# Attribute sums of a graph layer in groups of 32 nodes: two edges a product, destinations gathered and transposed

## The reference, cut to what matters

```python
h = jnp.maximum(_layernorm(x, axis=-1), 0.0)
x = x + _L0_gnn_ref(h, edge_index, W1, b1, W2, b2)     # two convolutions with D^-1/2 A D^-1/2
h = jnp.maximum(_layernorm(x, axis=-1), 0.0)
agg = jax.ops.segment_sum(edge_attr, col, num_segments=x.shape[0])   # (206250, 64) -> (6250, 64)
h = jnp.concatenate([h, agg, u[batch]], axis=1)        # then w1, w2, w3 with leaky relu
```

## Time and profile before

| | us |
|---|---|
| median of 3 runs | 1436.68 (1434.59 to 1437.53) |
| the profiled execution | 1436.67 |
| its span | 1435.0 |
| first stage | 0 to 148 |
| attribute stage | 148 to 415 |
| later stages | 415 to 1435 |

### The profile page before, as it was taken

One profiled execution on the slowest core, in us unless ns is written; L12 is line 12 of the kernel. 1 busy time (PEld: TensorE's weight loads), 2 busy tenths in 40 slices (PEclk: granted clock), 3 DMA queues, 4 the chain that ended last, 5 costly groups with the idle time before them and its releaser, 6 DMA issues. The chain is left out here.

```text
span 1435.0 us, 31864 instructions
## 1 busy us (share of the span) xinstructions
PE 1133.5 (79%) x10325; PEld 749.0 (52%) x10325; DVE 886.2 (62%) x1543; ACT 484.0 (34%) x1067; POOL 203.8 (14%) x170
## 2 busy tenths in 40 slices
PE   0012089999925889999999998549999999999974
PEld 0001089999924566666666664224444444444443
DVE  7575698888828979999999991621222222222221
ACT  0024100000006778888888882410111111111111
POOL 5710610000013922111111000300000000000000
PEclk9999999999966989999999999759999999999975
DMA  8423379999820545665446665959477777777400
GB/s 192 149 68 98 94 232 288 286 285 283 262 58 14 187 142 197 219 218 181 163 167 219 211 200 185 318 180 345 140 227 232 231 229 228 234 224 228 112 14 11
DMA packets 231891, 270.89 MB, mean 189 GB/s; under 512 B 31003, under 2 KB 202565, under 8 KB 231662
## 3 DMA queue, kind: packets, MB, share of 16 engines
q1 hardware_dynamic: 137258, 173.78, 39.5%
q10 hardware_dynamic: 89904, 81.89, 17.2%
q0 software_dynamic: 4688, 14.70, 3.3%
HBM read 178.73 MB, written 91.61 MB: 188 GB/s over the span
## 5 line engine op out<-in xcount | busy, mean ns | idle before, releaser
L779 ACT CAST adj_all<-win_p 128x392 f32 x784 | 346.9, 497 | 44.7 <-PE win_p L829 22.9
L829 PEld LDWEIGHTS win_p<-mv,st 128*128 128x128 f16 x3136 | 213.4, 100 | 141.8 <-ACT adj_all L779 21.7
L829 PE MATMUL win_p<-mv,st 128*128 128x98 f16 x3136 | 256.2, 211 | 17.9 <-ACT adj_all L779 10.7
L727 DVE TENSOR_TENSOR st<-iota_lo,code 128x2048 f16 x196 | 241.2, 1230 | 32.8 <-ACT code L768 13.2
L1369 PE MATMUL dense_p_b<-adj_all,g_hi 128*128 128x512 f16 (+1 forms) x637 | 232.2, 372 | 18.7 <-SPq L1127 16.6
L543 PE MATMUL agg_p<-ahot,arows 128*64 128x64 f32 x3724 | 218.8, 223 | 34.5 <-DVE ahot L584 34.5
L844 PE MATMUL dense_p<-adj_all,g_hi 128*128 128x448 f16 x686 | 241.5, 352 | 1.2 <-DVE total L738 0.8
L844 PE MATMUL dense_p<-adj_all,g_lo 128*128 128x448 f16 x686 | 242.1, 353 | 0.0
L543 PEld LDWEIGHTS agg_p<-ahot,arows 128*64 128x64 f32 x3724 | 218.7, 139 | 34.6 <-DVE ahot L584 34.6
L1369 PE MATMUL dense_p_b<-adj_all,g_lo 128*128 128x512 f16 (+1 forms) x637 | 232.1, 371 | 0.0
L727 DVE TENSOR_TENSOR mv<-iota_mv,code 128x1568 f16 x196 | 190.8, 973 | 0.0
(11 more groups left out here) (162 smaller groups left out, 1017.6 us busy)
## 6 DMA issues: line engine op xcount, KB each, us to landing
adj_d<-adj_all ACTq DMA_DIRECT2D x14, 5488.0 KB, 19.4
adj_all<-adj_d SPq DMA_DIRECT2D x11, 6272.0 KB, 23.5
arows<-in_edge_attr_dram SPq DMA_DIRECT2D x98, 608.0 KB, 3.6
adj_all<-adj_d SPq DMA_DIRECT2D x7, 896.0 KB, 9.9
disb<-dis_d SPq DMA_DIRECT2D x24, 256.0 KB, 4.9
hT_d<-hT ACTq DMA_DIRECT2D x12, 256.0 KB, 2.8
cur<-hT_d SPq DMA_DIRECT2D x12, 256.0 KB, 7.5
h1T_d<-total SPq DMA_DIRECT2D x12, 256.0 KB, 6.5
```

The costliest lines, as they stand in the source:

```text
L727: ins = nc.vector.tensor_tensor(hot[:, bass.ds((b * BG + j) % 2, 1), u, :, :] .rearrange("p a w (n t) -> p (a w) n t", t=2), iota[:, :].re ...
L779: nc.scalar.copy(adj[:, bass.ds(b % 2, 1), :, bass.ds(j * GN + k * WN, WN)] .rearrange("p b h d -> p (b h) d"), win_p[:, k % 4, 0:WP * MV] ...
L829: ins = nc.tensor.matmul(win_p[:, k % 4, 0:WP * MV] .rearrange("p (h c t) -> p h c t", c=WP, t=PN)[:, :, c, :], st[:, odd, k // UW, pair, ...
```

## The change

Groups have 32 nodes (196 of them, GA) and AC = 9 x 128 = 1152 edges, with a tenth column of zeros. A product takes two of a partition's edges at once: its 128 stationary columns are their 2 x 64 attributes, its 64 moving columns their two masks of 32 nodes; of the [128, 64] result the two diagonal blocks count, so that `agg` has 128 partitions, the upper and the lower half being parts of one sum. That makes 5 products a group. The two halves are summed by the perceptron's first product, whose weight `w1b` stands twice. Seven groups make a batch with one slot of four.

The destinations of all groups are gathered by two indirect transfers of GpSimd, one partition a group, in the first stage for the first round and in the attribute stage for the next; VectorE makes them relative, TensorE transposes them in 18 pieces, ScalarE stores them in `relT`. VectorE's loop in the attribute stage keeps the mask (one operation a batch) and two additions a batch. For this the starts of the groups are found early in the first stage, by counts of their own (L394 and L415 of the changed kernel). The counts of heads run in a loop. The degrees come from a shifting product on TensorE in place of the round trip through memory. Scaling h is ScalarE's, in ten parts.

In the diff below each "..." leaves lines out.

```diff
-AC = 19
+GA = 32
+NGA = NP // GA
+GP = NGA // 2
+AC = 9
+AP = AC + 1
+RC = 5
 ASLOTS = AC * P
+AU, AQ = 4, 7
+HR = 2
+RB = 6
 EF = 64
 
 EPR, EPC = 125, 1650
...
+        def gather_groups(pool, s_gathered):
+
+            for t in range(2):
+                pool.indirect_dma_start(
+                    out=adst[:, t, :], out_offset=None, in_=dst.rearrange("(e a) -> e a", a=1),
+                    in_offset=bass.IndirectOffsetOnAxis(ap=at_i[:, t:t + 1], axis=0)).then_inc(s_gathered, 16)
+
+        def place_groups(ch):
+
+            ch.link(nc.vector.tensor_scalar(at_f[:, :], want[:, :], float(E - ASLOTS), None, ALU.min))
+            ch.step(nc.vector.tensor_tensor(over[:, :], want[:, :], at_f[:, :], ALU.subtract))
+            return nc.vector.tensor_copy(at_i[:, :], at_f[:, :])
+
+        def offset_groups(ch, t):
+
+            ch.link(nc.vector.tensor_scalar(arel[:, t, :], pos[:, :], over[:, t:t + 1], BIG, ALU.is_lt, ALU.mult))
+            return nc.vector.scalar_tensor_tensor(out=arel[:, t, :], in0=adst[:, t, :], scalar=gbase[:, t:t + 1],
+                                                  in1=arel[:, t, :], op0=ALU.add, op1=ALU.add)
+
+        def turn_groups(t, c, n, to):
+
+            for k in range(n):
+                ins = nc.tensor.transpose(to[:, k * GP:(k + 1) * GP],
+                                          arel[:, t, :].rearrange("q (p c) -> q c p", c=AC)[:, c + k, :],
+                                          ident[0:GP, 0:GP])
+            return ins
...
+                pool.wait_ge(s_grows_i, 1)
+                for t in range(2):
+                    nc.gpsimd.indirect_dma_start(
+                        out=grows[:, t, :], out_offset=None, in_=dst.rearrange("(r c) -> r c", c=SR),
+                        in_offset=bass.IndirectOffsetOnAxis(ap=grow_i[:, t:t + 1], axis=0)).then_inc(s_grows, 16)
                 for k in range(HI):
                     if k % SB == 0:
                         pool.wait_ge(s_rows_i, k // SB + 1)
+                    if k == SB:
+                        pool.wait_ge(s_at, 1)
+                        gather_groups(nc.gpsimd, s_gathered)
+                    if k % SB == 0 and k >= RB * SB:
+                        pool.wait_ge(s_recounted, k - (RB - 1) * SB)
                     nc.gpsimd.indirect_dma_start(
-                        out=rows[:, k, :], out_offset=None,
-                        in_=dst.rearrange("(r c) -> r c", c=SR),
+                        out=rows[:, k % (RB * SB), :], out_offset=None, in_=dst.rearrange("(r c) -> r c", c=SR),
                         in_offset=bass.IndirectOffsetOnAxis(ap=row_i[:, k:k + 1], axis=0)).then_inc(s_rows[k // SB], 16)
...
+                for t in range(2):
+                    ch.step(nc.vector.tensor_scalar(cmp[0:GP, t, :], heads_b[0:GP, :], tgtg[:, t:t + 1], None,
+                                                    ALU.is_lt, ALU.add, accum_out=gcnt[:, t:t + 1]))
+                ch.wait()
+                ch.link(nc.vector.tensor_scalar(gcnt[:, :], gcnt[:, :], -1.0, 0.0, ALU.add, ALU.max))
+                nc.vector.tensor_copy(grow_i[:, :], gcnt[:, :]).then_inc(s_grows_i, 1)
+
+                def count_rows(b):
+                    for k in range(SB):
+                        nc.vector.tensor_scalar(cmp[:, k, :], heads_b[:, :], tgt[:, bass.ds(b * SB + k, 1)], None,
+                                                ALU.is_lt, ALU.add, accum_out=cnt[:, bass.ds(b * SB + k, 1)]
+                                                ).then_inc(s_counted, 1)
+                    ks = bass.ds(b * SB, SB)
+                    gate(dve, s_counted, b * SB + SB)
+                    nc.vector.tensor_scalar(cnt[:, ks], cnt[:, ks], -1.0, 0.0, ALU.add, ALU.max).then_inc(s_row_f, 1)
+                    gate(dve, s_row_f, b + 1)
+                    nc.vector.tensor_copy(row_i[:, ks], cnt[:, ks]).then_inc(s_rows_i, 1)
+
+                count_rows(0)
+
+                dve.wait_ge(s_grows, 32)
+                for t in range(2):
+                    ch.step(nc.vector.tensor_scalar(cmp[0:GP, t, 0:SR], grows[:, t, :], tgtg[:, t:t + 1], None,
+                                                    ALU.is_lt, ALU.add, accum_out=gcnt2[:, t:t + 1]))
+                ch.wait()
+                ch.link(nc.vector.scalar_tensor_tensor(out=want[:, :], in0=gcnt[:, :], scalar=float(SR),
+                                                       in1=gcnt2[:, :], op0=ALU.mult, op1=ALU.add))
+                place_groups(ch).then_inc(s_at, 1)
+
+                with dve.Fori(1, HI // SB) as b:
+                    count_rows(b)
...
+                dve.wait_ge(s_gathered, 32)
+                for t in range(2):
+                    offset_groups(ch, t).then_inc(s_arel, 1)
...
+                dve.wait_ge(s_small_p, 5)
+                nc.vector.tensor_copy(next_sb[:, :], next_p[:, :]).then_inc(s_next, 1)
+                dve.wait_ge(s_next, 1)
+                ch.link(nc.vector.tensor_tensor(deg[:, :], next_sb[:, :], cnt[:, 0:HI], ALU.subtract))
+                nc.vector.tensor_scalar(deg[:, :], deg[:, :], 1.0, 1.0, ALU.add, ALU.max).then_inc(s_var, 1)
+                dve.wait_ge(s_var, 2)
...
+            rows = sb("arows", [P, AU, AQ, AP, EF], F32, ph)
+            hot = sb("ahot", [P, HR, AQ * AP, GA], F32, ph)
+            agg = sb("agg", [P, NP], F32, ph)
...
+                for q, (k, n) in enumerate(SPLIT):
+                    pool.wait_ge(s_hi, q + 1)
+                    nc.gpsimd.tensor_tensor(g_lo[:, k:k + n, :], scaled[:, q % 2, 0:n, :], g_hi[:, k:k + n, :],
+                                            ALU.subtract).then_inc(s_lo, 1)
...
+                with pool.Fori(0, rounds) as r:
+                    gate(pool, s_at, r + 2)
+                    gather_groups(nc.gpsimd, s_gathered)
...
-                    with sp.Fori(0, NG // AU) as i:
+                    with sp.Fori(0, TURNS) as i:
                         for k in range(AU):
-                            at = sp.value_load(at_i[0:1, bass.ds(AU * i + k, 1)], min_val=0, max_val=E - ASLOTS)
-
-                            sp.wait_ge(s_summed, (r * (NG // AU) + i) * AU + (k + 1))
-                            sp.dma_start(rows[:, k, :, :].rearrange("p c f -> p (c f)"),
-                                         attr[bass.ds(at, ASLOTS), :].rearrange("(p c) f -> p (c f)", p=P)
-                                         ).then_inc(s_loaded[k], 16)
-                            sp.dma_start(adst[:, k, :],
-                                         dst[bass.ds(at, ASLOTS)].rearrange("(p c) -> p c", p=P)
-                                         ).then_inc(s_loaded[k], 16)
+                            for q in range(AQ):
+                                at = sp.value_load(at_row[0:1, bass.ds(r % 2, 1), bass.ds((i * AU + k) * AQ + q, 1)]
+                                                   .rearrange("a b c -> a (b c)"), min_val=0, max_val=E - ASLOTS)
+                                if q == 0:
+
+                                    sp.wait_ge(s_summed, (r * TURNS + i) * AU + (k + 1))
+                                sp.dma_start(rows[:, k, q, 0:AC, :].rearrange("p c f -> p (c f)"),
+                                             attr[bass.ds(at, ASLOTS), :].rearrange("(p c) f -> p (c f)", p=P)
+                                             ).then_inc(s_loaded[k], 16)
...
+                def sum_batch(r, i, k):
+                    n = (r * TURNS + i) * AU + k + 1
+                    pe.wait_ge(s_loaded[k], (r * TURNS + i + 1) * (16 * AQ))
+                    pe.wait_ge(s_hot, n)
+                    pe.wait_ge(s_added, n)
+                    for q in range(AQ):
+                        for c in range(0, AP, 2):
+                            ins = nc.tensor.matmul(agg_p[:, k, q * 2 * GA:(q + 1) * 2 * GA],
+                                                   rows[:, k, q, c:c + 2, :].rearrange("p c f -> p (c f)"),
+                                                   hot[:, k % HR, q * AP + c:q * AP + c + 2, :]
+                                                   .rearrange("p c n -> p (c n)"),
+                                                   start=(c == 0), stop=(c == AP - 2))
+                    ins.then_inc(s_summed, 1)
+
                 with pe.Fori(0, rounds) as r:
-                    with pe.Fori(0, NG // AU) as i:
+                    with pe.Fori(0, TURNS // 2) as i:
                         for k in range(AU):
-                            pe.wait_ge(s_loaded[k], (r * (NG // AU) + i + 1) * 32)
-                            pe.wait_ge(s_hot, (r * (NG // AU) + i) * AU + (k + 1))
-                            pe.wait_ge(s_added, (r * (NG // AU) + i) * AU + (k + 1))
-                            for c in range(AC):
-                                ins = nc.tensor.matmul(agg_p[k][:, :], rows[:, k, c, :], hot[:, k, c, :],
-                                                       start=(c == 0), stop=(c == AC - 1))
-                            ins.then_inc(s_summed, 1)
```

(94 more changed lines are left out.)

393 lines of the change are left out of this document (212 added, 181 removed).

## The result

The changed kernel takes 1615.66 us (median of four runs) against 1435.63 of the kernel before in the same comparison: a ratio of 1.126, 95% interval 1.124 to 1.128. Forecast were 1436.4 us and a range of 1417 to 1450. The kernel is **180 us slower**.

A forecast was written before the change was run, and what follows sets the result against it. TensorE was taken to bound the attribute stage before the change, SyncE's queue after it. The sum was 1436.7 - 3.2 (attribute stage) + 1.5 (store) + 0.5 (last stage) + 0.9 (first stage) = 1436.4 us, range 1417 to 1450.

The forecast's parts named there:

- The sums on TensorE: Attribute stage: 1960 weight loads at 0.11 us each, 216 us in all, against 218.8 before.
- The upper bound of the step: Attribute products: load and stream end to end, 0.11 + 0.053 us a record, 320 us in all.
- SyncE's queue: Attribute stage: transfers 1.20 us apart, 237.5 us, become the bound; store of the sums 3.2 us earlier.
- rival D: SyncE's queue in the attribute stage: pitch 1.30 us, stage 19.5 us longer, 1456 us in all; chance 0.12.
- The start of the stage: Attribute stage: the 16.0 us wait for positions is gone; first issue moves from 166.80 to 150.8.
- The stall in mid-stage: Attribute stage: TensorE waits 8 us (4 to 12) for the next round's offsets, at no net cost.
- Storing the sums: After the attribute stage: agg's store from 128 partitions takes 11.1 us, +1.5; bounds 9.6 and 9.6 + 7.8.
- The last stage: One more weight transfer ahead of the adjacency loads, +0.5 us.
- The first stage: Up to the attribute stage: shift 7.9 us later, tail 7.0 us shorter, together +0.9; bounds -17.6 and +9.7.
- the shift: First stage, the normalization's shift, paced by VectorE: at 102.5 us where it was 94.61, +7.9.
- the hole: First stage: VectorE gets through little from 50 to 84 us, taken to last as long as GpSimd's gathers run.
- rival C: First stage: the hole stays whole and added work comes on top, +9.7 us, 1445 in all; chance 0.14.

The follow-up runs named there:

- e1_twice: Changed kernel with each attribute product given its 64 moving columns twice, so 128 move; 1420.7 us, ratio 1.0075 to the kernel before.
- e3_wake: Changed kernel with twelve fp32 products of 512 columns ahead of the first attribute product; 1591.1 us (one run).
- e4: Changed kernel with groups of 64 nodes instead of 32, still two edges a product, 128 moving columns; 1407.9 us, ratio 0.9985 to the kernel before.
- e2: Kernel before with 32 of the 64 moving columns of each attribute product, leaving out half the sums; 1585.9 us (one run) against 1408.8.
- e6: e4 with one edge a product again, 64 stationary and 64 moving columns; 1394.0 us, ratio 0.989 to the kernel before.
- e5_rows128: Kernel before with agg and w1b in 128 partitions, the upper half of agg zero; 1399.1 us, ratio 0.993 to the kernel before.
- a_again: Changed kernel run again without further change; 1596.2 us (one run), ratio 1.132 to the kernel before.

## Why the prediction was wrong, point by point

- **The sums on TensorE: the step that failed.** "So the load sets the pitch ... I take 0.11" was a price at 2.4 GHz, from rows of 966 and 1018 us. It measured 0.112 in e1_twice, and in the first 70 records of e3_wake, and 0.213 in the changed kernel, 418.6 us in place of 216. I took it for granted that TensorE would come up to 2.4 GHz in this stage because it did before. It is the form of the products that decides. With 64 loaded and 64 moved columns (before), and with 128 and 128 (e1, e4), TensorE rises; with 128 loaded and 64 moved (the change, e3) or 64 and 32 (e2) it does not, and in e3 it falls from the upper level. e1 and e2 change the moving columns alone, in the two directions. Which property of these forms counts, the columns moved or the results written, no run separates. The upper bound of the step, a load and a stream end to end (320 us), was itself reckoned at the upper level, so even the range could not hold the result. The Trainium skill (TensorE: Matmul & The Clock Gate, What's actually happening) says that the lower clock is the default and that activity releases it. That agrees with the 0.107 us of the first 25 records before and should have been weighed as a rival. By that sentence alone the changed kernel would have risen too: its records leave no gap from 185 to 344 us, and the gauge still finds the lower level at 344.7.
- **SyncE's queue.** The reasoning was right and the size a little off: e1_twice, with TensorE out of the way, is paced by it at 1.295 us a transfer where 1.20 (1.22 with waits and turns) was taken; 252.6 us for 237.5. That is rival D's pitch, 1.30. In the changed kernel none of it shows: SyncE waits for TensorE.
- **The start of the stage.** The first transfer was put 2.1 us behind the stage's start; 2.4 were measured (151.64 to 154.06). The 16 us for positions are gone, as forecast.
- **The stall in mid-stage.** In the changed kernel 8.6 us lie between the two products around it, for 8 (4 to 12) forecast, but it has no clock to lose there. At the upper level that was too little: 12 to 15 in e4 and e6, since TensorE falls to 0.50 in it and rises again only after it (250.7 us in e6, 5 us behind the first product).
- **Storing the sums.** 9.2 us to land and not 11.1, just under the lower bound of 9.6: +1.5 was not there. The nearest row was a transfer of another kind.
- **The last stage** was forecast at +0.5 and came at -12.5 (474.9 to 462.5 us). The step named the extra weight transfer only and did not ask what the height of the operand does to TensorE. e5_rows128 shows 9 of it; the rest is open.
- **The first stage.** In the first profiles the shift came at 103.08 for 102.5 forecast, and VectorE was at full pace soon after the last gather, as supposed. Together it is +3.0 for +0.9: 0.6 by the shift and 1.5 by a longer tail. In runs without the hole it was rival C's figure, 9.7 forecast and 10.0 measured, but by luck: C had the hole stay whole. The rows shown come from one execution and could not tell that there are runs without it.
- **The rivals.** None had the cause. D ends on the right side by another mechanism and for a ninth of the size (19.5 us of 180).

## What to carry to other kernels

A price for an fp32 product is a pair, one at each level of the clock (here 0.107 and 0.058 us a record for 64 loaded columns, 0.213 and 0.112 for 128), and a change to its shape can decide which one holds. Before halving a count of products, look for the load and the stream of the new form at both levels, and do not use a granted clock of 1.00 ahead of the trace's first clock record: use a known operation's duration. Where a stage runs at half clock with a busy TensorE, giving its products more columns to move can be worth more than the work costs (e1_twice against a_again: 1.0075 and 1.132 times the kernel before).

## What the runs showed that I had not expected

- More work was faster: the moving columns given twice took the group of products from 418.6 to 228.2 us, and half of them taken away (e2_half) cost 177 us.
- TensorE dropped to the 0.50 level at 159.1 us and stayed there to the end of the stage, at work without a gap from 160 to 318 us (e3_wake).
- Holding one operand of a mixed chain of products in 128 partitions instead of 64, with zeros above, is worth 9 to 10 us of 1409 here (e5_rows128). Its price lies in the gaps between records more than in their busy time.
- VectorE's 28 us hole in the first stage was there in the first profiles and in none of the later ones. What makes it stays open, and nothing was tried against it.
- The preparation of a next round that never comes may cost twice: beside the stall in mid-stage, attributes come late while its gathers run (a gap of 6.1 us in e1_twice).
